# Routed expert tiles of a GNN + mixture-of-experts kernel: the order of a tile's small steps on three engines, and one weight split done in two pieces

## What is computed

```python
sh = gelu(einsum('td,sdh->sth', xf, sW1) + sb1)            # 2 shared experts, 256 hidden
shared = (einsum('sth,shd->std', sh, sW2) + sb2).mean(0)
gates = xf @ rW + rb;  top-2 of 8 experts, softmax -> w
h = gelu(einsum('td,edh->eth', xf, W1) + b1)               # 8 routed experts, 256 hidden
y = einsum('eth,ehd->etd', h, W2) + b2
out = x + shared + einsum('te,etd->td', w, y)
```

## Time and profile before

| | |
|---|---|
| median of three runs | 335.24 us (333.43 to 336.17) |
| the profiled execution | 334.91 us |
| its span, first to last instruction | 333.0 us |
| granted TensorE clock | 0.999 of full |
| TensorE matmul busy | 317.9 us, 95% |
| TensorE weight load busy | 274.6 us, 82% |
| VectorE busy | 241.2 us, 72% |
| ScalarE busy | 188.3 us, 57% |
| GpSimd busy | 80.2 us, 24% |

### The profile page before, as it was taken

How to read it: one execution, slowest core, us unless ns; L and a number is a source line. 1 busy time by engine, 2 the same in 40 slices (tenths; PEclk the granted TensorE clock), 3 DMA queues, 4 the chain that set the end, 5 groups by cost and what they waited for, 6 DMA issues and landing times.

```text
span 333.0 us, 6122 instructions
## 1 busy us (share of the span) xinstructions
PE 317.9 (95%) x1994; PEld 274.6 (82%) x1994; DVE 241.2 (72%) x466; ACT 188.3 (57%) x315; POOL 80.2 (24%) x94
## 2 busy tenths in 40 slices
PE   6999999999999999999999999999999999999994
PEld 2889897787799888879989887897788878878874
DVE  2999999976747537845565879768787677480885
ACT  2896999993130323433166897776787678640000
POOL 6641180001010010110213431222144230004840
PEclk9999999999999999999999999999999999999999
DMA  8960013000010145396231595697889972134994
GB/s 246 353 186 2 2 58 116 1 2 17 0 63 3 63 174 190 119 325 261 80 113 65 156 349 190 228 361 296 278 290 338 389 303 112 74 131 159 311 337 180
DMA packets 27014, 57.60 MB, mean 173 GB/s; under 512 B 2735, under 2 KB 16541, under 8 KB 26984
## 3 DMA queue, kind: packets, MB, share of 16 engines
q1 hardware_dynamic: 20458, 33.89, 29.5%
q0 software_dynamic: 3888, 14.16, 12.7%
q10 hardware_dynamic: 2638, 9.17, 7.3%
HBM read 66.25 MB, written 14.03 MB: 241 GB/s over the span
## 4 chain that ended last, share of the span: by engine, by line
PE 48%; ACT 17%; DMA 14%; DVE 8%; issue 6%; POOL 3%; SPq 1%; ACTq 1%; POOLq 1%; DVEq 0%
PE ps L1485 27%; PE ps L1773 6%; PE ps L1609 6%; ACT sw_raw L823 6%; DMA y_acc<-in_x 4%; DMA raw<-in_L_ffn_W 3%; POOL big L664 3%; DMA big<-in_L_ffn_W 3%; DMA big<-yrow,at_i 3%; PE ps L1762 2%; ACT arena_r L758 2%; ACT sw_raw L831 2%; PE ps L1495 2%; DVE xt L1409 2%; DVE arena_r L1389 1%
## 5 line engine op out<-in xcount | busy, mean ns | idle before, releaser
L1485 PE MATMUL ps<-arena_r 128*128 128x512 f32 (+1 forms) x264 | 67.3, 401 | 0.2 <-DVE arena_r L1184 0.2
L1485 PE MATMUL ps<-xt,arena_r 128*128 128x314 f32 (+3 forms) x324 | 60.3, 337 | 0.0
L1485 PE MATMUL ps<-arena_r,xt 128*128 128x286 f32 (+1 forms) x360 | 59.0, 305 | 0.3 <-DVE arena_r L535 0.3
L655 POOL DMA_INDIRECT big<-xrow,tok_i x17 | 34.2, 2011 | 95.9 <-PE ps L1762 76.8
L1485 PEld LDWEIGHTS ps<-arena_r 128*128 128x128 f32 (+1 forms) x264 | 48.0, 188 | 11.0 <-DVE arena_r L1184 0.6
L1485 PEld LDWEIGHTS ps<-xt,arena_r 128*128 128x128 f32 (+1 forms) x324 | 51.2, 187 | 5.5 <-issue 0.2
L1485 PEld LDWEIGHTS ps<-arena_r,xt 128*128 128x128 f32 (+1 forms) x360 | 49.2, 187 | 1.3 <-DVE arena_r L535 0.5
L1389 DVE TENSOR_TENSOR arena_r<-raw,arena_r 128x2048 fp32r<-128x2048 f32 x17 | 38.8, 2284 | 1.6 <-ACT arena_r L985 1.5
L1773 PE MATMUL ps<-big,tile 128*128 x160 | 37.5, 380 | 0.2 <-issue 0.2
L985 ACT ACTIVATE arena_r<-raw 128x2048 fp32r x17 | 32.5, 1910 | 8.0 <-DMA raw<-in_L_ffn_W 4.7
L1773 PEld LDWEIGHTS ps<-big,tile 128*128 128x128 f32 x160 | 29.9, 189 | 5.5 <-issue 1.1
(11 more groups left out here) (234 smaller groups left out, 463.8 us busy)
## 6 DMA issues: line engine op xcount, KB each, us to landing
big<-in_L_ffn_W SPq DMA_DIRECT2D x19, 1024.0 KB, 7.3
raw<-in_L_ffn_W SPq DMA_DIRECT2D x19, 1024.0 KB, 9.9
yrow<-work ACTq DMA_DIRECT2D x17, 512.0 KB, 3.1
raw<-in_L_gnn_W_rel SPq DMA_DIRECT2D x2, 1144.0 KB, 10.8
y_acc<-in_x SPq DMA_DIRECT2D x4, 512.0 KB, 8.2
xrow<-work SPq DMA_DIRECT2D x4, 512.0 KB, 2.9
raw<-in_L_ffn_sW SPq DMA_DIRECT2D x2, 1024.0 KB, 5.8
sw_raw<-in_L_ffn_sW SPq DMA_DIRECT2D x2, 1024.0 KB, 11.8
```

What stands on the lines that cost most here:

```text
L655: pool.indirect_dma_start(xg[i % 2], None, xrow, bass.IndirectOffsetOnAxis(tok_i[:, i:i + 1], 0)) \
L1485: ins = pe.matmul(out_ap, a, b, start=start and k == 0, stop=stop and k == n - 1)
```

## The change

Four edits. `tile_hidden(i + 1)` moves behind `tile_down(i)` on TensorE, but for `i` = 15. `keep_y_act(i)` moves ahead of `tile_gelu(i + 1)` on ScalarE, but for `i` = 15. `keep_y(i)` moves ahead of `tile_lo(i + 1)` on VectorE, but for `i` = 15. The split of the first shared W2 is cut in two halves of 1024 columns, in iterations 1 and 2 of ScalarE and 2 and 3 of VectorE; the second stays whole where it was.

```diff
-        SW2_AT = (1, NT - 3)
+        SW2_HALVES, SW2_AT = (1, 2), NT - 3
...
+                if i != NT - 2:
+                    keep_y_act(i)
                 if i + 1 < NT:
                     tile_gelu(i + 1)
+                if i == NT - 2:
+                    keep_y_act(i)
                 if i + 2 < NT:
                     w2_hi(i + 2, ring_next)
-                keep_y_act(i)
                 store_y(i)
-                if i in SW2_AT:
-                    split_hi(SW2_AT.index(i), True)
+                if i in SW2_HALVES:
+                    half = SW2_HALVES.index(i)
+                    raw_v, hi_v, _ = unit_views(0, True)
+                    act.wait_ge(s_sw2, 16)
+                    act.activation(hi_v[:, half], raw_v[:, half], ACT.Copy).then_inc(s_hi if half else s_sw2h, 1)
+                if i == SW2_AT:
+                    split_hi(1, True)
...
+                if i == NT - 2:
                     tile_lo(i + 1)
                 keep_y(i)
-                if i - 1 in SW2_AT:
-                    split_lo(SW2_AT.index(i - 1), True)
+                if i < NT - 2:
+                    tile_lo(i + 1)
+                if i - 1 in SW2_HALVES:
...
+                    ins = dve.tensor_tensor(lo_v[:, half], raw_v[:, half], hi_v[:, half].bitcast(F32), ALU.subtract)
+                    if half:
+                        ins.then_inc(s_lo, 1)
+                if i - 1 == SW2_AT:
+                    split_lo(1, True)
...
-                if i + 1 < NT:
-                    tile_hidden(i + 1)
                 if i == 1:
                     pe.wait_ge(f_g, 4)
+                if i == NT - 2:
+                    tile_hidden(i + 1)
                 tile_down(i)
+                if i < NT - 2:
+                    tile_hidden(i + 1)
```

More of the change, by code:

```diff
@@ L354, in program @@
         s_half = sem("s_halflo")
+        s_sw2h = sem("s_stwohalf")
         s_gd = sem("s_gd")
@@ L502, in _ @@
                              w2v[bass.ds(e, 1)].rearrange("e p k n -> (e p) k n"), cond=new).then_inc(s_w2[i % 2], 16)
-                if i == SW2_AT[1] - 1:
+                if i == SW2_AT - 1:
                     load_sw2(1)
@@ L1433, in _ @@
                         w1_lo(i + 2, ring_next)
+                if i == NT - 2:
                     tile_lo(i + 1)
                 keep_y(i)
-                if i - 1 in SW2_AT:
-                    split_lo(SW2_AT.index(i - 1), True)
+                if i < NT - 2:
+                    tile_lo(i + 1)
+                if i - 1 in SW2_HALVES:
+                    half = SW2_HALVES.index(i - 1)
+                    raw_v, hi_v, lo_v = unit_views(0, True)
+                    if half == 0:
+                        dve.wait_ge(s_sw2h, 1)
+                    else:
+                        dve.wait_ge(s_hi, U_SW2 + 3 - NLN)
+                    ins = dve.tensor_tensor(lo_v[:, half], raw_v[:, half], hi_v[:, half].bitcast(F32), ALU.subtract)
[3 more added lines that the diff above has]
+                    split_lo(1, True)
                 if i == 6:
```

## The result

The changed kernel takes 333.31 us, the median of 20 runs (332.06 to 336.23), against 335.29 of 20 runs of the kernel before beside it. The ratio is 0.9941, interval [0.9916, 0.9966]; forecast was 333.2, which is 0.994. In a second measurement it was 0.9918 [0.9881, 0.9954]. The sum was right. Its terms were not all right, as the profile shows at once.

A forecast was written before the change was run, and what follows sets the result against it. TensorE's own work, 7.03 us per undisturbed tile, plus its waits at five places was taken as the bound. Gains 0.95 + 0.65 + 0.50 less 0.05 made 2.05: 335.24 to 333.2 us, range 331.2 to 335.4.

The forecast's parts named there:

- The sum: Whole change: 0.95 + 0.65 + 0.50 - 0.05 = 2.05 us gained, from 335.24 to 333.2 us.
- A: Tile at 202.40 to 210.38: TensorE waits for `keep_u` behind the whole shared W2 split; the wait disappears, gain 0.95 us.
- Two reasons of which either would do: At A: transposes moved behind the 2.78 us down, or half a split ahead of `keep_u`; either removes the wait.
- The undisturbed tile stays at 7.03: Loop tiles without waits on TensorE: row-transpose distance stays 7.03 us; moved transposes cost 0.
- the bound of 0.11: Border between down and moved transposes: at most one such transpose, 0.11 us each; 15 would make 1.6.
- C: Tile at 232.21 to 240.26, late W2 load: rows' copy right behind W2's rounding, gain 0.65 us, between 0.5 and 0.8.
- E: Tile at 269.11 to 276.64, same as C: no wait is left, gain 0.50 us.
- B: Tile at 224.45 to 232.21: ScalarE's `w1_hi` waits for a weight load, excess 0.73 us; gain 0.
- D: Tile before 269.11: W1 load holds `w1_hi` until 265.04, excess taken as B's; gain 0.
- The stores leave about a microsecond earlier; nobody waits for them.: Stores after `keep_y` moves ahead of `tile_lo`: leave earlier, with nobody waiting inside the loop.
- Rival 1: Loads don't move along, earlier stores compete on the DMA engines; D swallows A and C: 334.8 us, chance 0.13.
- ScalarE's longer chain, 0.97 to spare: GELU and `w2_hi` now behind the down's copy: next rounded up still ready 0.97 us early, cost 0.

## Why the prediction was right, point by point

The time came out because errors of both signs met, which is luck in part. Term by term:

- **A, 0.95.** Right in size: 7.96 and 7.04 at A in the two kernels without loads. "Two reasons of which either would do" is wrong: I followed `keep_u` only as far as the transposes and not on to `w2_lo` and `w1_lo`, behind which TensorE waits next. The halves do it, the transposes alone move the wait.
- **The undisturbed tile stays at 7.03.** Almost: 7.04. The border between down and transposes costs 0.01 a tile, well inside the bound of 0.11.
- **C and E, 0.65 and 0.50.** The mechanism was right: the next rows' copy now follows W2's rounding at once, and from `w2_hi` to the rounded up E is shorter by 0.67. At C it is shorter by only 0.32, since `w2_lo` started 0.49 behind the rounding and not 0.15. But I read the price from one execution in which the waits for loads cost 2.98, where they cost 4.25 at the median, and the copies are worth 2.5 and not 1.15. Beyond this chain the profiles show loads that land in time, and that is not explained.
- **B and D, 0, each landing moves with its issue.** Wrong as a rule, and the step that failed. The W2 load at C was issued 1.08 earlier and landed 0.74 later, the W1 load at B 1.07 earlier for 0.55, and B went from 7.76 to 8.27, D from 7.75 to 7.18. How late a load is depends on the bytes beside it: two experts in successive tiles, and the stores' 0.5 MB.
- **"The stores leave about a microsecond earlier; nobody waits for them."** True of the store, but the sentence leaves out the loads beside it, which are waited for: a store 2.7 later than the changed kernel's costs it 2.1 at the median. Rival 1, where an early store was to collide with the loads, has the other sign. What the 1.2 us are worth by which the change itself sends stores out earlier was not measured; with ScalarE's copy alone, 1.85 were had without them.
- **ScalarE's longer chain, 0.97 to spare.** Nothing contradicts it: with no late load every tile from tile 2 on is level at 7.04.
- **The sum.** 2.05 forecast, 1.98 measured in the first measurement and 2.5 in the second. The copies alone gave 1.35 more than reckoned and the halves alone 0.85 more than A; all edits together give hardly more than the copies. How far the moved transposes take it back, which I had at nothing, and how far it is scatter, stays open. A sum that comes out does not prove its terms.

## What to carry to other kernels

When the bound engine waits for loads, look at what else is on the DMA engines at that moment, other loads and stores alike: here four weight loads within 9.5 us were late enough to hold up TensorE only with the stores' 0.5 MB per tile beside them, and delaying those stores made the kernel slower. A wait for a transfer that one profile shows is one draw; its price is the median with the transfer against the median without it. And two edits that are to remove the same wait should be timed singly and together, since the second may bring only its cost.

## What the runs showed of the hardware

- With stores of 64 KB in place of 512 KB the share of busy DMA engines fell only from 0.97 to 0.84 and the rate from 345 to 285 GB/s, and yet no load held up TensorE any more; what ScalarE still waited for loads (2.6 us in the loop, where it was 6.9) was hidden. So a share of 0.97 was already too much here, and 0.84 was not.
- A store's issue on ScalarE's queue costs ScalarE nothing behind a long activation that is still running (186.60 and 186.63 above). Behind a copy whose completion is awaited it costs 0.94 with the register load.
- From the last row transposes to the end of the span the profiles with the halved split take 0.4 less (332.4 - 283.51 = 48.9 after, 333.0 - 283.68 = 49.3 before). With full stores it is 48.8 to 49.16 in the profiles with halves and 49.15 to 49.7 in those without. Between before and after the difference lies in the last gather, 8.36 and 7.92 us on the chain of waits; what that has to do with the halves, if anything, is open.
